# Setup scales from sums of squares, and the pipeline's first slots written out by hand

## What is computed

```python
ln = layernorm(x); x = x + attention(ln, ln, ltor_mask) @ w_ao + b_ao
ln = layernorm(x); x = x + attention(ln @ w_q, ctx @ w_kv, cross_mask) @ w_co + b_co
x = x + gelu(layernorm(x) @ w1 + b1) @ w2 + b2
# second block: x are the latents, ctx the input
q = x @ q_w + q_b; k, v = concat(ctx, x) @ kv_w + kv_b
a = softmax(where(mask, q k / 16, -inf)) v @ out_w + out_b + x
out = gelu(rmsnorm(a) @ mlp_w1 + mlp_b1) @ mlp_w2 + mlp_b2 + x
```

## Time and profile before

| | before |
|---|---|
| median of 3 runs | 1186.29 us |
| the profiled execution's own time | 1186.25 us |
| its span, first to last instruction | 1184.4 us |
| TensorE busy | 1095.9 us (93%) |
| VectorE busy | 1006.4 us (85%) |
| ScalarE busy | 961.1 us (81%) |
| GpSimd busy | 558.9 us (47%) |
| mean granted TensorE clock | 0.958 |

### The profile page before, as it was taken

The page is one execution under the profiler, slowest core; times in us unless marked ns, Lnnn a source line. Parts: engine busy times, 40 slices in busy tenths (PEclk is TensorE's granted clock), DMA queues, the critical chain, the costliest instruction groups (busy, mean ns, idle before and its releaser), DMA issues.

```text
span 1184.4 us, 46509 instructions
## 1 busy us (share of the span) xinstructions
PE 1095.9 (93%) x19440; PEld 952.5 (80%) x19440; DVE 1006.4 (85%) x2462; ACT 961.1 (81%) x2137; POOL 558.9 (47%) x749
## 2 busy tenths in 40 slices
PE   3765688999999999999999999999999999999987
PEld 2644577788888888888888888888888888888866
DVE  6877877888989888888889898888888988988763
ACT  1364577888888889898888888899888888888876
POOL 0352454455554554545555445445455454554330
PEclk9556799999999999999999999999999999999999
DMA  7321100000000000000000000000000000000000
GB/s 271 141 108 48 48 13 14 14 13 4 13 18 18 19 19 18 18 19 18 13 8 19 19 19 18 18 18 19 18 19 13 8 19 18 27 7 7 7 6 20
DMA packets 29858, 34.12 MB, mean 29 GB/s; under 512 B 11856, under 2 KB 27984, under 8 KB 29136
## 3 DMA queue, kind: packets, MB, share of 16 engines
q1 hardware_dynamic: 29648, 31.14, 8.1%
HBM read 26.93 MB, written 4.19 MB: 26 GB/s over the span
## 4 chain that ended last, share of the span: by engine, by line
PE 57%; POOL 15%; DVE 13%; issue 9%; ACT 5%; DMA 1%; POOLq 0%; SPq 0%; DVEq 0%; ACTq 0%
PE psum L423 23%; PE psum L599 10%; PE psum L436 6%; PE psum L559 6%; PE psum L397 4%; POOL prob_self L1476 4%; PE psum L526 4%; PE psum L545 3%; POOL xb L1453 3%; POOL ctxT L1416 3%; DVE prob_self L1013 2%; ACT xn_mlp L1247 1%; POOL ctx_lo L1424 1%; POOL rstd_mlp L1431 1%; POOL ctx_hi L1418 1%
## 5 line engine op out<-in xcount | busy, mean ns | idle before, releaser
L1476 POOL TENSOR_TENSOR prob_self<-prob_self,add_self 128x512 f32<-128x512 f32 x64 | 80.3, 1275 | 178.3 <-DVE prob_self L1013 178.3
L1476 POOL TENSOR_TENSOR prob_cross<-prob_cross,add_cross 128x512 f32<-128x512 f32 x64 | 80.1, 1272 | 86.0 <-DVE prob_cross L1013 86.0
L1319 ACT ACTIVATE staging<-psum,cols,down 128x128 f32<-128x128 f32 x256 | 95.8, 453 | 6.2 <-PE psum L423 5.7
L1319 ACT ACTIVATE hid_mlp<-psum,folded,down 128x128 f32<-128x128 f32 x256 | 97.0, 471 | 3.3 <-PE psum L423 3.2
L599 PE MATMUL psum<-hi_n,staging 128*128 128x256 f16 x512 | 94.6, 273 | 4.0 <-DVE staging L1074 4.0
L423 PE MATMUL psum<-xT_mlp,hi_m 128*128 128x128 f16 x1024 | 96.1, 223 | 0.0
L599 PE MATMUL psum<-hi_m,parts_mlp 128*128 128x256 f16 x512 | 95.9, 276 | 0.0
L423 PE MATMUL psum<-xT_mlp,hi_n 128*128 128x128 f16 x1024 | 92.6, 219 | 0.4 <-DVE xT_mlp L950 0.3
L423 PE MATMUL psum<-xT_mlp,lo_m 128*128 128x128 f16 x512 | 92.2, 223 | 0.0
L423 PE MATMUL psum<-xT_mlp,lo_n 128*128 128x128 f16 x512 | 89.1, 219 | 0.0
L1431 POOL TENSOR_TENSOR rstd_cross<-var_cross,minus_half 128x1 f32<-128x1 f32 x32 | 17.6, 551 | 149.8 <-DVE var_cross L944 149.8
(11 more groups left out here) (320 smaller groups left out, 4129.1 us busy)
## 6 DMA issues: line engine op xcount, KB each, us to landing
late<-in_ctxT SPq DMA_DIRECT2D x2, 2048.0 KB, 7.3
xin<-in_x SPq DMA_DIRECT2D x32, 128.0 KB, 2.1
ctxT<-in_ctxT SPq DMA_DIRECT2D x32, 128.0 KB, 2.1
late<-in_x SPq DMA_DIRECT2D x2, 2048.0 KB, 7.4
out<-xb SPq DMA_DIRECT2D x32, 128.0 KB, 2.2
staging<-in_w_m SPq DMA_DIRECT2D x2, 1024.0 KB, 5.1
staging<-in_w_n SPq DMA_DIRECT2D x2, 1024.0 KB, 5.2
mask<-in_mask_cross SPq DMA_DIRECT2D x32, 32.0 KB, 2.0
```

The costliest lines, as they stand in the source:

```text
L1319: last = e.activation(hid[t][g][:, j * P:(j + 1) * P], ps[:, j * P:(j + 1) * P], ACT.Gelu_apprx_tanh, bias=b1[:, 4 * g + j:4 * g + j + 1], ...
L1476: e.tensor_tensor(ch, ch, over_heads(a[:, :]), ALU.add).then_inc(sem["added_" + t], 1)
```

## The change

Four things are done.

**Scales from sums.** ScalarE squares each weight with the sum per partition as a second output (`squares_of`, `squares_of_tile`, `squares_of_bias`, `squares_of_part`), TensorE adds the partitions by a product with a tile of ones (`total`), and VectorE makes the powers for a whole group of items at once from the exponent of that sum, halved (`powers`, `scale_of`). `q`, `out`, `kv` and the second block's weights (`lat`) form one group, `mid`. The context keeps its largest value, on VectorE. VectorE no longer takes a maximum over the weights, except one over 128x1536 (`largest_lat`).

**Work moved.** The products of scales (`undone`), `key_bias`, `bias_spread`, `ones_beside` and `add_mask` go from VectorE to GpSimd. The low halves of `m1`, `m2` and `side` go from GpSimd to VectorE (with the scale applied there), and ScalarE no longer rewrites these three in place. `n1` and `n2` stay as they were.

**The first slots.** On each engine a list of single calls with fixed units stands ahead of the loop: 146 calls on TensorE, 199 on VectorE, 124 on ScalarE, 82 on GpSimd, 23 on SyncE. They hold all the setup and, of the units, self up to unit 3 (qkv and scores' operands of unit 4 too), cross of units 0 to 2 (scores of 3), mlp0 of 0 to 2, ctx/lat of 0 and 1. Their TensorE calls have banks of their own.

**The loop.** It starts at slot `FILL` = 7 of `SLOTS` = 42. All units' offsets are 2 larger, the body is rotated to begin with the scores of `self`, it has nearly the same order, and some calls have other banks.

```diff
-SLOTS = UNITS + 12
+SLOTS = UNITS + 10
+FILL = 7
...
+            @once
+            def total(group, b):
+                items = SCALED_TOGETHER[group]
+                q.wait_ge("constants", ONES)
+                q.wait_ge(*steps(group, len(items)))
+                ps = claim(b, ("total", group), *steps(group, len(items) + 2))
+                here = slice(item(items[0]), item(items[0]) + len(items))
+                for part in range(PARTS):
+                    last = e.matmul(ps[:, 0:len(items)], ones[:, :], sums[:, part, here], start=(part == 0), stop=(part == PARTS - 1))
+                last.then_inc(sem[STEPS_OF[group]], 1)
...
+            def scale_of(at, n, src, root):
+                ex, inverse = exponent[:, 0, at:at + n], exponent[:, 1, at:at + n]
+                from_zero = F32_BIAS + TOP + (F32_BIAS - 1) // (2 if root else 1) - (1 if root else 0)
+                alone(e.tensor_scalar(ex, src.bitcast(I32), F32_MANTISSA + (1 if root else 0), None, ALU.logical_shift_right))
+                alone(e.tensor_scalar(ex, ex, -1, from_zero, ALU.mult, op1=ALU.add))
+                alone(e.tensor_scalar(ex, ex, F32_BIAS + REACH, F32_BIAS - REACH, ALU.min, op1=ALU.max))
+                alone(e.tensor_scalar(inverse, ex, -1, 2 * F32_BIAS, ALU.mult, op1=ALU.add))
+                return e.tensor_scalar(power[:, :, at:at + n].bitcast(I32), exponent[:, :, at:at + n], F32_MANTISSA, None,
+                                       ALU.logical_shift_left)
...
+            def square(junk, src, scale, name, part):
+                return e.activation(junk, src, ACT.Square, scale=scale, accum_out=sum_at(name, part))
...
-                    alone(e.tensor_reduce(row_top[:, :], w[name][:, :, :], AX.X, ALU.max, apply_absolute_value=True))
-                    alone(e.tensor_tensor(row_top[:, :], row_top[:, :], col(ROW_SCALE[name], 0, KH), ALU.mult))
...
+            moments(0, "self")
+            powers(0, "qkv")
+            two_heads(0)
+            folded_bias(0, "qkv")
+            low_half(0, "self")
+            low_weight(0, "qkv")
+            largest_part(0, 0)
+            q_bias_self(0)
+            k_spread(0, "self", 0)
+            k_spread(0, "self", 1)
+            moments(1, "self")
+            masked(0, "self", 0)
...
+            for t in range(FILL, SLOTS):
+                shifted(t - 4, "cross", 1)
+                lat_low(t - 5)
+                denominators(t - 6, "lat")
+                masked(t - 3, "self", 0)
...
+            load_columns(0)
+            load(0)
+            load_weight(0, "qkv")
+            load(1)
+            load_part(0, "ctx", 0)
+            load_tile(0, "out")
+            load_mask(0)
+            load_weight(0, "q")
+            load_tile(0, "side")
```

More of the change, by code:

```diff
@@ new lines, in _ @@
+            total(0, "qkv", 3)
+            qk_self(0, 2)
+            through(0, "ao", 3)
+            score_bank(0, "self", 4)
+            score(0, "self", 0)
+            v_self(0, 5)
+            total(0, "mid", 4)
+            turn(1, "self", 7)
+            fold(0, "q", 3)
+            prob_turn_bank(0, "self", 5)
+            qk_self(1, 3)
+            through(0, "co", 7)
+            fold(0, "m1", 2)
+            top_turn(0, "ctx", 4)
+            prob_turn(0, "self", 1)
+            top_spread(0, "ctx", 4)
@@ new lines, in _ @@
+            moments(0, "self")
[10 more added lines that the diff above has]
+            masked(0, "self", 0)
+            largest_lat(0)
+            masked(0, "self", 1)
+            largest_score(0, "self", 0)
+            powers(0, "mid")
@@ new lines, in _ @@
+            largest_score(2, "cross", 1)
+            lat_low(0)
+            moments(1, "mlp0")
+            heads_low(3, "self")
+            k_spread(3, "cross", 0)
+            k_spread(3, "cross", 1)
+            q_bias_lat(0)
+            shifted(2, "cross", 1)
+            add_residual(3, "self")
+            masked(0, "ctx", 0)
+            moments(3, "cross")
+            low_half(1, "mlp0")
+            k_spread(0, "lat", 0)
+            k_spread(0, "lat", 1)
+            masked(0, "ctx", 1)
@@ new lines, in squares_of_tile @@
+            @once
+            def squares_of_tile(tile):
+                q.wait_ge("ld_" + tile, 16 * len(TOGETHER[tile]))
+                if tile == "out":
+                    for k, name in enumerate(("ao", "co")):
+                        last = square(w_hi[name][:, :, :], w[name][:, :, :], 1.0, "out", k)
+                else:
+                    for k in range(KH):
+                        last = square(w_hi["side"][:, k, 0:2 * H], w["side"][:, k, 0:2 * H], 1.0, "kv", k)
+                last.then_inc(sem["steps_mid"], 1)
@@ new lines, in hidden_hi @@
+                q.wait_ge("undone", UNDONE[t])
+                e.activation(part[t][g][:, 0:512], hid[t][g][:, :], ACT.Copy, scale=hidden_up[t]).then_inc(sem["hid_hi_" + t], 1)
+            normalize(0, "self")
+            squares_of(0, "qkv")
+            high_half(0, "self")
+            high_weight(0, "qkv")
+            squares_of(0, "q")
+            squares_of_tile(0, "out")
+            squares_of_tile(0, "side")
+            normalize(1, "self")
+            high_side(0, "out")
+            values(0, "self")
@@ new lines, in key_bias @@
+            @once
+            def key_bias(t):
+                q.wait_ge("ld_cols", 16)
+                q.wait_ge("two_heads", 1)
+                if t == "self":
+                    q.wait_ge("fold_add", FOLDED.index("qkv") + 1)
+                src = {"self": folded[:, KH:2 * KH], "cross": col("b_kv", 0, KH), "lat": col("k_b", 0, KH)}[t]
+                for i in range(HC):
+                    last = e.tensor_scalar(bias_of_two[t][:, i, :], src, head_of_two[:, i:i + 1], None, ALU.mult)
+                last.then_inc(sem["bias_of_two"], 1)
@@ new lines, in _ @@
+            undone(0, "qkv")
+            ones_beside(0, "self")
+            mask_add(0)
+            ones_beside(0, "cross")
+            add_mask(0)
+            key_bias(0, "self")
+            key_bias(0, "cross")
+            bias_spread(0, "ao")
+            root(1, "self")
+            added(0, "self", 0)
+            mask_keys(0)
+            ones_beside(0, "lat")
+            added(0, "self", 1)
+            key_bias(0, "lat")
+            plus_bias(0, "self")
+            undone(0, "out")
```

1432 lines of the change are left out of this document (887 added, 545 removed).

## The result

The changed kernel takes 1149.2 us (median of 4 runs, 1149.08 to 1150.44); the kernel before took 1186.4 beside it. The ratio is 0.9692, 95% interval [0.9675, 0.9708]: 37.1 us less. The profiled execution took 1149.08 us, its span 1147.3.

The account below looks back on a forecast made before the run. TensorE bounds the steady part; VectorE's work and waits bound the filling. A 13 us start plus 145 puts unit 4's self masking at 158, 46.2 us earlier; the rest adds 0: 1186.25 - 46.2 = 1140.0 us, range 1122 to 1164.

Parts of the forecast that it names:

- five signs with bounds: Unit 4's self masking 150–166; VectorE busy 122–132 before it; first qkv product 17–20; slot 32.3–32.9; masking to end 975–985 us.
- the mark: VectorE's self masking of unit 4, end of the compared first part: from 204.17 to 158 us, 46.2 earlier.
- the first product: TensorE's first qkv product: at about 18 us and not at 27.55.
- B: Rival, first part: TensorE bounds it because its clock stays low; 1157 or 1176 us; chance 0.10.
- A: Rival, first part: VectorE and GpSimd exclude each other on shared memory, three stalls each; 1156 us; chance 0.12.
- The start: VectorE's start before real work, qkv's landing and its squares: about 13 us.
- total and powers: Step between qkv's squares and its high half, on the way to the first product: 1.6 us.
- VectorE's work: VectorE's work up to unit 4's self masking: 157.4 us less 30.2, so 127 us.
- idle share: VectorE's waits up to unit 4's self masking: busy 87.5%, near the steady stretch's, so 127 us of work take 145.
- C: Rival, steady loop: later-freed banks slow each slot; 1.7 us per slot cancels the gain, 2.1 gives 1198; chance 0.05.
- D: Rival, first part: limited by chains of one unit, only a third of VectorE's 30 us saved; 1167 us; chance 0.08.
- E: Rival, better case: VectorE at 93% in the first part and 0.2 us per slot; 1125 us; chance 0.07.

Follow-up runs that it names:

- pad: Changed kernel plus idle work on one engine, early or late: VectorE 1153.8, 1155.0 us; ScalarE 1149.2, 1154.8; TensorE 1152.1, 1151.0.
- e5_old_work: Changed kernel with 21.1 us of useless VectorE work (scans, single-column copies) put back at the old places, new list order kept: 1169.8 us.
- e1_slots: New scales and moved work, but slot order, banks and DMA list of the kernel before: 1183.1 us, against 1186.4 before.
- e3_chunks: Changed kernel with GpSimd's subtractions over n1 and n2 each cut into eight instructions: 1145.7 us.
- e2_low_on_pool: Changed kernel with low halves of m1, m2 and side back on GpSimd, their in-place scaling back on ScalarE: 1160.0 us.
- VectorE's pad: Changed kernel plus one idle 4.4 us reduction on VectorE near 41 us, its result unread: 1153.8 us.
- TensorE's early pad: Changed kernel with unit 0's twelve small cross-key products near 51 us repeated three times more: 1152.1 us.
- e4_sync: Changed kernel with SyncE's DMA list of the kernel before, all else as changed: 1179.9 us.

## Why the prediction held, and where it was off

**The time.** 1140 was forecast, 1149.2 measured, inside the range. The forecast's own range (1128 to 1152) holds it too. 46.2 us of gain were foreseen, 37.1 came. All five signs with bounds came within them, the mark (165.2 of 150 to 166) and the first product (19.8 of 17 to 20) at the late end. The clock of 1.00 by 90 us, which would have spoken against B, didn't come; one long VectorE row beside a GpSimd subtraction, A's sign, did. One reading was off without harm: TensorE's strip is at 9 from the eighth slice, so seven slices are low (207 us), not eight.

**The start.** Foreseen: real work from 13 us, first product at about 18. Measured: 14.78 and 19.80. The step that failed is "total and powers", 1.6 us, right behind the squares. TensorE's list has `fold` of qkv ahead of `total`. The chain of waits of the changed kernel:

```profile
8.96 4.93 PE psum L366 x24
13.89 0.87 PE psum L379 x4
16.00 1.77 ACT hi_qkv L1429 x2
```

The 24 fold products take 4.93 us, and the sums were read off at 10.5. From there to the high half at 16.00 it is 5.5 us for 1.6. I priced `total` and not what it is queued behind. That the product came only 1.3 us later than my sum (18.5) is luck: qkv's landing, which I had counted at 11, as before, was at about 8.5, and its squares were done at 10.5 and not at 13.2. `total` ahead of the fold was not run.

**VectorE's work.** 127 us foreseen, 128.4 measured, 29.0 less than before for 30.2. One long row beside a GpSimd subtraction is in it (4.50), as the one at 124.10, which the count kept, was in the work of before (4.57). **ScalarE's**: 120 foreseen, 116.4 measured. **GpSimd's**: 76 foreseen, 82.7 measured. Its small steps on scales took 0.21 to 1.17 each (a memset of 128x544 0.55) and not the 0.19 of its product of two columns. ScalarE has slack early and none late, so what its error was worth is not shown, nor is GpSimd's.

**The idle share.** Foreseen 12.5% of the time behind the start, 18 us; measured 150.4 - 128.4 = 22.0 us, 14.6% (0.8 us of the work lies ahead of the start, by this count and by mine). This is the largest mis-sized term. The steady stretch's share was the wrong neighbour: there TensorE alone has hardly any idle time, while here VectorE, TensorE and late ScalarE all pass on 0.8 to 1.4 of a pad's length to the mark. The sum: 1.8 for the start, 1.4 for the work, 4.0 for the idle time, and 1.9 behind the mark, 9.1 in all.

**What the saved work is worth.** The prediction took 30 us of VectorE's work at more than its full length, in one sum with the order. e5_old_work puts it at near its full length in the new order (20.6 for 21.1), and e1_slots refutes it for the old one (3.3 for 33). What I called VectorE's bound before the mark in the old kernel was not one: at 77% busy it had 46.8 us of idle time, and removing work made more of it. The two parts are no sum. The forecast holds because the change has both.

**The DMA list.** The prediction gave it a share in the first product's 9 us, and called side and out covered. It saw neither that the queue stands where a buffer isn't free, nor that the scan's place in VectorE's list decides for how long. The old DMA list under the new engine lists costs 30.7 us: 11.6 of them are the later start, 11.1 the wait for the mask and what follows it, and the other 8 come between the first masking and the end. In the changed kernel the second part is issued at 24.10, as the first scan ends, with the mask and all that is needed early ahead of it.

**Rivals.** A: its mechanism was there, once and not three times, at 3.5 us (e3_chunks); the second long subtraction, at 147.20, met no row. VectorE's row began 0.11 us behind GpSimd's (89.24 and 89.13) and ended 0.55 behind it (93.74 and 93.19), as if it had run, at its usual 0.68, only when the other was done. The Trainium skill's "SBUF — State Buffer" (section "Who interferes with whom") says that a VectorE instruction with two SBUF inputs contends with a GpSimd instruction that reads SBUF; these rows agree. The cost is the collision's, not the work's, since e2_low_on_pool had three more such subtractions and no more collisions.

B: the clock did stay at 0.72 to 0.73 from 18 to 110 us, as B said. But the clock was not the bound up to 60 us: at 1.00 there VectorE's pad still cost its length. From 60 to 110 us that kernel had 0.73 as well, so B is not tested there. TensorE's early pad cost 3.1 us for 3.9, so B was off in size more than in kind.

C: the slot is 32.62 against 32.60, no loss.

D: refuted for the change as a whole, yet e1_slots fits D's picture for the old slots: units came in when the slot said so (self maskings of units 0 to 4 at 36.96, 77.0, 123.0, 164.6, 198.2), however little VectorE had to do. Which chain set that pace no run shows. In the changed kernel they stand at 26.1, 56.1, 76.4, 103.8 and 165.2.

E: no.

## What to carry to other kernels

An engine that is 77% busy in a pipeline's filling, and the fullest, need not be its bound: 33 us less work on it moved the end by 3, and the same kind of work was worth its full length once the lists were rewritten. The DMA queue is one of these lists: a load that waits for a buffer holds all loads behind it, so its place must go with the place of whatever frees the buffer, and it is changed together with the engines' lists. The same holds for work moved to another engine: where it stands in that engine's list can cost more than the work (e2_low_on_pool, 10.8 us). A long GpSimd subtraction cut into pieces let VectorE's row beside it through: 1145.7 against 1149.2 (ratios to before 0.9664 [0.9644, 0.9683] and 0.9692 [0.9675, 0.9708]; the intervals overlap, so the gain is likely and not sure, while the long row is gone).

## What the runs showed of the hardware

- DMAs issued behind large ones land late: the 24 KB of `cols` took 8.7 us to land as the fourth, behind the 2 MB (e4_sync), and 1.7 as the first; qkv's 768 KB took 8.7 right behind the 2 MB and 4.7 ahead of them.
- A DMA whose buffer isn't free holds those behind it in SyncE's list: none was issued from 12.8 to 35.7 us in e4_sync.
- A square with a sum costs ScalarE little more than a plain pass: 1.14 us for 128x1024 where a scaled copy of that size took 1.15 (0.93 for 128x768, 3.6 for 128x4096). The row that reads the sum is 0.19 long, and the next square starts before its end (8.53, 9.46).
- Eight subtractions of 128x256 on GpSimd took 5.97 us beside VectorE's rows and 5.08 at 144 us, where no VectorE row was longer than in the changed kernel; one of 128x2048 took 4.06 to 4.08. So a cut cost 0.14 us in the second place.
- 24 products of a 128x128 float32 tile with a single column took TensorE 4.93 us.
